# Transfers of 106 rows split into 96 and 10, the input loaded in three parts, edge columns and one-hots moved

## The reference, cut to what matters

```python
def _rgcn_conv(x, edge_index, edge_type, W, root, bias):
    src, dst = edge_index
    x_src = x[src]
    out = x @ root + bias
    for r in range(4):
        mask = (edge_type == r).astype(x.dtype)
        s = segment_sum(x_src * mask[:, None], dst, num_segments=6250)
        c = segment_sum(mask, dst, num_segments=6250)
        out = out + (s / jnp.maximum(c, 1.0)[:, None]) @ W[r]
    return out
# three layers, relu after the first two; then
x = layernorm(x + network(x))
```

## Time and profile before

| | |
|---|---|
| median of 3 runs | 2091.7 us (2090.06 to 2094.24) |
| the profiled execution, its time | 2091.99 us |
| its span | 2090.2 us |
| granted clock of TensorE, mean | 0.879 |
| busy: TensorE, VectorE, ScalarE, GpSimd | 1652.7, 1359.6, 1141.2, 1480.7 us |
| GpSimd's share of the chain that ended last | 40% |

### The profile page before, as it was taken

The page is one execution under the profiler, slowest core; times in us unless marked ns, Lnnn a source line. Parts: engine busy times, 40 slices in busy tenths (PEclk is TensorE's granted clock), DMA queues, the critical chain, the costliest instruction groups (busy, mean ns, idle before and its releaser), DMA issues.

```text
span 2090.2 us, 29086 instructions
## 1 busy us (share of the span) xinstructions
PE 1652.7 (79%) x8296; PEld 1169.6 (56%) x8296; DVE 1359.6 (65%) x4230; ACT 1141.2 (55%) x1679; POOL 1480.7 (71%) x1459
## 2 busy tenths in 40 slices
PE   6702657788899999769999988987769999997743
PEld 3402544344456666547876655655458777775543
DVE  4797866799999988424259988876234252446752
ACT  4511000144566788367858768776367677664500
POOL 1088778877777777647777777777377777777774
PEclk9955666799999999889999999999879999999855
DMA  6411222133344455487855445444488777763431
GB/s 204 159 34 34 72 61 64 58 127 104 124 140 147 157 175 188 135 276 248 269 161 172 169 146 177 159 160 162 139 274 261 236 247 249 238 217 105 142 89 51
DMA packets 169224, 330.76 MB, mean 158 GB/s; under 512 B 34704, under 2 KB 85648, under 8 KB 169060
## 3 DMA queue, kind: packets, MB, share of 16 engines
q1 hardware_dynamic: 119000, 230.27, 31.8%
q0 software_dynamic: 46400, 94.97, 16.2%
q10 hardware_dynamic: 3660, 3.60, 0.7%
HBM read 210.05 MB, written 118.65 MB: 157 GB/s over the span
## 4 chain that ended last, share of the span: by engine, by line
POOL 40%; DVE 21%; PE 18%; issue 14%; DMA 3%; DVEq 1%; ACTq 1%; ACT 1%; SPq 0%; POOLq 0%
POOL ring L796 40%; DVE V L1505 5%; DVE S L1452 4%; PE psB L1043 4%; PE psD L1043 3%; DVE V L1504 3%; DMA ring<-ytab,idxc 2%; PE psY L838 2%; PE psGR L961 2%; PE psRB L961 1%; DVE rows L1300 1%; DVE node L1474 1%; DVEq L1460 1%; DMA hrows<-yst 1%; PE psT L838 1%
## 5 line engine op out<-in xcount | busy, mean ns | idle before, releaser
L796 POOL DMA_INDIRECT ring<-ytab,idxc x1402 | 1410.5, 1006 | 576.1 <-issue 419.7
L1043 PE MATMUL psD<-afull,xs 128*128 128x512 f32 (+1 forms) x1862 | 618.6, 459 | 30.3 <-ACT afull L1128 11.8
L1452 DVE TENSOR_SCALAR S<-odd_f,relc,wc 128x129 f32<-128x129 f32 x1450 | 480.6, 398 | 29.3 <-PE psGR L961 20.3
L1128 ACT ACTIVATE afull<-aring 128x1024 fp32r<-128x1024 f16 (+1 forms) x375 | 367.3, 1032 | 126.5 <-PE psD L1043 54.9
L1043 PEld LDWEIGHTS psD<-afull,xs 128*128 128x128 f32 (+1 forms) x1862 | 359.5, 198 | 96.3 <-ACT afull L1178 20.0
L1505 DVE TENSOR_SCALAR V<-odd_h,recs 128x513 f16<-128x513 f16 x686 | 325.0, 474 | 0.0
L961 PE MATMUL psRB<-S,ring 128*128 128x128 f32 (+1 forms) x1440 | 224.6, 305 | 102.6 <-DMA ring<-ytab,idxc 90.5
L1178 ACT ACTIVATE afull<-psT 128x512 fp32r<-128x512 f32 x355 | 205.2, 593 | 179.6 <-PE psT L1059 177.7
L1182 ACT ACTIVATE aring<-afull 128x1024 f16<-128x1024 f32 x275 | 286.1, 1040 | 25.5 <-ACT afull L1178 0.7
L961 PE MATMUL psGR<-S,ring 128*128 128x128 f32 x1364 | 212.4, 306 | 102.3 <-DMA ring<-ytab,idxc 93.0
L961 PEld LDWEIGHTS psRB<-S,ring 128*128 128x128 f32 (+1 forms) x1440 | 205.3, 214 | 131.6 <-issue 86.4
(11 more groups left out here) (207 smaller groups left out, 1580.8 us busy)
## 6 DMA issues: line engine op xcount, KB each, us to landing
aring<-a_dram SPq DMA_DIRECT2D x180, 512.0 KB
a_dram<-aring SPq DMA_DIRECT2D x132, 512.0 KB
ytab<-yst SPq DMA_DIRECT2D x144, 256.0 KB
ring<-ytab,idxc POOLq DMA_INDIRECT x1402
hrows<-yst SPq DMA_DIRECT2D x96, 64.0 KB
yst<-hrows SPq DMA_DIRECT2D x24, 256.0 KB, 4.6
yst<-in_x SPq DMA_DIRECT2D x23, 256.0 KB, 4.2
out<-yst SPq DMA_DIRECT2D x11, 256.0 KB, 2.7
```

Of the source, the lines that this page charges most:

```text
L796: e.indirect_dma_start(rows_at(n, i, m), None, Y[li % 2], bass.IndirectOffsetOnAxis(ap=idxc[0:m, t:t + 1], axis=0)).then_inc(landed(n), 16)
L1043: last = e.matmul(bank[:], xs[0:m, s, i, :], a, start=(i == 0 and s == 0), stop=(i == NB - 1 and s == 1))
L1128: e.activation(afull[:, n % AF, 0:m, :], aring[:, cc % AS, o:o + m, :], ACT.Copy).then_inc(q["s_cv"], 1)
L1452: last = e.tensor_scalar(run3(S[:, n % NS, i, 0:P + 1]), odd128f, relc[:, t:t + 1], wc[:, t:t + 1], ALU.is_equal, ALU.mult)
```

## The change

- Each transfer of 106 rows (stores of the table and of `hrows`, loads of x, stores of the output) is made in two: rows 0 to 95 and rows 96 to 105 (`row_parts`, `z_moves`).
- x is loaded in three parts: blocks 0 to 7 and 8 to 19 by ScalarE's queue, blocks 20 to 47 and the 106 rows by SyncE's, after the edges and ahead of the constants. The biases have a semaphore of their own, and ScalarE does a small copy right after the identity has landed.
- Edge columns are turned after blocks 0, 2 and 4. TensorE's products for phase 0 come after block 17, the transposes of the edge scans' ends after block 28, the places of phase 0 after block 39, the carries after block 41. VectorE does the edge scans' first half before the scan of phase 0. Phase i+1 is counted before the places of phase i are taken.
- The mask of phase 0 lies in the gather ring, so GpSimd's first gather also waits for the scan of phase 0.
- `ohs` is built for four pairs by one `tensor_tensor` in f16 (by its columns interleaved by four), `ohk` as before. `recs` is split in two tensors.
- START_PE goes from 205 to 177, START_POOL from 95 to 89.

```diff
-START_PE, START_POOL = 205.0, 95.0
+START_PE, START_POOL = 177.0, 89.0
...
+    batch_of, batches = {}, []
+    for v, (w, _, _) in enumerate(pairs):
+        if not batches or len(batches[-1]) == 4 or pairs[batches[-1][0]][0] != w:
+            batches.append([])
+        batch_of[v] = (len(batches) - 1, len(batches[-1]))
+        batches[-1].append(v)
...
+        mask0 = ring[:, 0:(scn + 1) // 2].bitcast(F16)
...
-        nxt0 = min(8, NB - 2)
+        nxt0, nxt1 = min(8, NB - 3), min(20, NB - 2)
+        row_parts = lambda m: [(a, b) for a, b in ((0, m // 16 * 16), (m // 16 * 16, m)) if b > a]
...
-            e.dma_start(Y[li % 2][NR * P * k:NR * (P * k + bw[k]), :].rearrange("(n r) f -> n (r f)", r=NR),
-                        yst[0:bw[k], n % YS, 0:NR * D]).then_inc(s_yd[n % YS], 16)
+            for a, b in row_parts(bw[k]):
+                e.dma_start(Y[li % 2][NR * (P * k + a):NR * (P * k + b), :].rearrange("(n r) f -> n (r f)", r=NR),
+                            yst[a:b, n % YS, 0:NR * D]).then_inc(s_yd[n % YS], 16)
...
 def sync_engine(e):
             load_tail(e, a_typ, typ, q["s_e0"])
+            k = N // P
+            e.dma_start(xn[:, nxt1:k, :], x[nxt1 * P:k * P, :].rearrange("(k p) f -> p k f", p=P)).then_inc(q["s_x2"], 16)
+            for a, b in row_parts(N - k * P):
+                e.dma_start(xn[a:b, k, :], x[k * P + a:k * P + b, :]).then_inc(q["s_x2"], 16)
             e.dma_start(iota[:], c_iota).then_inc(q["s_k0"], 16)
...
 def gpsimd_engine(e):
             e.wait_ge(q["s_tev"], 1)
+            e.wait_ge(q["s_prod"], 1)
             y_stored(e, 0)
...
 def tensor_engine(e):
-            e.wait_ge(q["s_w0"], 48)
+            e.wait_ge(q["s_w0"], 32)
...
+                if k == 0:
+                    pe_cols(e, a_idx, ("s_idx", 1))
                 if k == min(2, NB - 1):
-                    pe_cols(e, a_idx, ("s_idx", 1))
-                if k == min(6, NB - 1):
                     e.wait_ge(q["s_tev"], 1)
                     pe_cols(e, a_dstf, ("s_dst", 1))
-                if k == min(8, NB - 1):
+                if k == min(4, NB - 1):
                     e.wait_ge(q["s_tev"], 2)
                     pe_cols(e, a_rel, ("s_dst", 1))
-                if k == min(24, NB - 1):
+                if k == min(17, NB - 1):
                     pe_rank(e, 0)
-                if k == min(40, NB - 1):
+                if k == min(28, NB - 1):
+                    e.wait_ge(q["s_tev"], 3)
+                    e.wait_ge(q["s_end"], 1)
...
+                if k == min(39, NB - 1):
                     pe_places(e, 0)
+                if k == min(41, NB - 1):
...
 def scalar_engine(e):
-            e.dma_start(bt[:], biases.rearrange("l o -> o l")).then_inc(q["s_w0"], 16)
-            nf = N // P
-            e.dma_start(xn[:, nxt0:nf, :], x[nxt0 * P:nf * P, :].rearrange("(k p) f -> p k f", p=P)).then_inc(q["s_x1"], 16)
-            if nf < NB:
-                e.dma_start(xn[0:bw[-1], NB - 1, :], x[nf * P:N, :]).then_inc(q["s_x1"], 16)
+            e.dma_start(bt[:], biases.rearrange("l o -> o l")).then_inc(q["s_b"], 16)
+            e.dma_start(xn[:, nxt0:nxt1, :], x[nxt0 * P:nxt1 * P, :].rearrange("(k p) f -> p k f", p=P)).then_inc(q["s_x1"], 16)
+            e.wait_ge(q["s_c"], 16)
+            e.activation(sd[:, 0:1], ident[:, 0:1], ACT.Copy)
...
 def vector_engine(e):
             rank_counts(0)
...
-            rank_scan(0)
-            records()
-            rank_places(0)
...
             e.sem_inc(q["s_end"], 1)
+            rank_scan(0)
             e.wait_ge(q["s_tp"], 4)
...
             e.sem_inc(q["s_car"], 1)
+            records()
+            rank_places(0)
             e.wait_ge(q["s_tp"], 5)
...
-            for i in range(1, len(pl.phases)):
-                rank_counts(i)
-                rank_scan(i)
-                rank_places(i)
+            for i in range(1, NPH + 1):
+                if i < NPH:
+                    rank_counts(i)
+                if i > 1:
+                    rank_places(i - 1)
+                if i < NPH:
+                    rank_scan(i)
...
 def onehots(upto):
-                    e.tensor_scalar(run3(ohs[:, v % NO, :]), odd128, recs[:, 0, at:at + 1], None, ALU.is_equal)
-                    e.tensor_scalar(run3(ohk[:, v % NO, :]), odd512, recs[:, 1, at:at + 1], None, ALU.is_equal
+                    if not first:
+                        m = len(batches[n])
+                        e.tensor_tensor(ohs[:, n % NQ, :, 0:m], by4(irep[:, 0:4 * P])[:, :, 0:m],
+                                        recr[:, at:at + m].unsqueeze(1).to_broadcast([P, P, m]), ALU.is_equal)
+                    e.tensor_scalar(run3(ohk[:, v % NO, :]), odd512, reck[:, at:at + 1], None, ALU.is_equal
                                     ).then_inc(q["s_oh"], 1)
```

More of the change, by code:

```diff
@@ L639, in z_plan @@
             for b, ks in enumerate(lasts):
-                parts = 1 if (bw[ks[-1]] == P or len(ks) == 1) else 2
+                parts = len(z_moves(ks))
                 total[b % NZ] += 16 * parts
@@ L677, in x_load @@
                     e.wait_ge(q["s_xw"], n - YS + 1)
-                for a, c, rr in z_parts(ks):
-                    e.dma_start(yst[0:rr, n % YS, a * P:c * P].rearrange("p (k f) -> p k f", f=D),
-                                node_rows(h_dram[l], ks[a], c - a, rr)).then_inc(s_xs[n % YS], 16)
+                for a, c, r, s in z_moves(ks):
+                    e.dma_start(yst[r:s, n % YS, a * P:c * P].rearrange("p (k f) -> p k f", f=D),
+                                node_rows(h_dram[l], ks[a], c - a, r, s)).then_inc(s_xs[n % YS], 16)
             y_stored(e, 0)
@@ L718, in store @@
                     e.wait_ge(q["s_no"], b + 1)
-                    for a, c, rr in z_parts(it[1]):
-                        e.dma_start(node_rows(out, it[1][a], c - a, rr), zx[0:rr, b % NZ, a:c, :]).then_inc(s_z[b % NZ], 16)
+                    for a, c, r, s in z_moves(it[1]):
+                        e.dma_start(node_rows(out, it[1][a], c - a, r, s), zx[r:s, b % NZ, a:c, :]).then_inc(s_z[b % NZ], 16)
                     if b + NZ - 1 < len(lasts):
@@ L1058, in pe_chunk @@
                     e.wait_ge(q["s_oh"], v + 1)
-                    e.matmul(tbank(u)[:], ohs[:, v % NO, 0:P], ohk[:, v % NO, 0:NR * P], start=(j == 0),
+                    e.matmul(tbank(u)[:], ohs[:, batch_of[v][0] % NQ, :, batch_of[v][1]], ohk[:, v % NO, 0:NR * P], start=(j == 0),
                              stop=(j == c - 1)).then_inc(q["s_bd"], 1)
@@ L1500, in onehots @@
                     w, i, j = pairs[v]
-                    if v >= NO:
-                        e.wait_ge(q["s_bd"], v - NO + 1)
                     at = pl.slot0[w] + i * pl.win[w][2] + j
-                    e.tensor_scalar(run3(ohs[:, v % NO, :]), odd128, recs[:, 0, at:at + 1], None, ALU.is_equal)
-                    e.tensor_scalar(run3(ohk[:, v % NO, :]), odd512, recs[:, 1, at:at + 1], None, ALU.is_equal
+                    used = v - NO + 1
+                    n, first = batch_of[v]
+                    if not first and n >= NQ:
+                        used = max(used, batches[n - NQ][-1] + 1)
+                    if used > 0:
+                        e.wait_ge(q["s_bd"], used)
+                    if not first:
[3 more added lines that the diff above has]
+                    e.tensor_scalar(run3(ohk[:, v % NO, :]), odd512, reck[:, at:at + 1], None, ALU.is_equal
                                     ).then_inc(q["s_oh"], 1)
```

75 lines of the change are left out of this document (41 added, 34 removed).

## The result

The changed kernel takes 2058.3 us in the median of four runs (2056.5 to 2060.2), the kernel before 2091.4 beside it; the ratio is 0.984, with a 95% interval from 0.9826 to 0.9854. The forecast was 2079.6, with a range from 2065 to 2093. The direction was right; the gain of 33 us is nearly three times the forecast's 12, and the time lies outside the range.

A forecast was written before the change was run, and what follows sets the result against it. GpSimd's gathers, 1.25 us each at best, with the first gather's time, their stretching, two layer gaps and the tail set the time: -4.0 -4.2 -7.3 -8.2 -1.0 +12.6 = -12.1, so 2079.6 us beside the median, range 2065 to 2093.

The forecast's parts named there:

- First gather, -8.2: Start of the kernel: GpSimd's first gather moves from 100.68 to about 92.5 us, -4.0 and -4.2.
- Its two parts: Before the first gather: (a) the split store of the 106-row block, -4.0; (b) blocks coming earlier, -4.2.
- Edge scans, -7.3: First gathers: VectorE's edge scans come earlier and stretch fewer gathers, -7.3 us, between -3 and -7.9.
- the gathers up to 124.9 would lie near 945: Sign at the start of layer 0: these gathers, 1510 ns in the mean before, would take near 945 ns.
- Gaps, -8.2: Two gaps between layers: split 106-row stores save 4.2 us in the first, 4.0 in the second; from -3 to -9.
- the shifted planner constants: Order of layer 0: worth 0, with -3 to +3 for output blocks more or fewer after its last gather.
- Tail, -1.0: End of the kernel: the output's last 106-row transfer is split, -1.0 us, from 0 to -1.8.
- One-hots, +12.6: Gathers: 179 new tensor_tensor hold them 0.07 us each, +12.6 us in all; ends +3 and +25.
- VectorE is relieved of 114 us, off the path: worth 0: VectorE: one-hots fall from 189 us to 75 us, and this relief changes nothing in the time.
- Rival 1: Gathers: the new tensor_tensor hold hardly any, 0.02 us each, +3.5 in all; time 2071 us; chance 19%.
- Waits in layer 0, 0: GpSimd in layer 0: no term for waits for others; gathers waiting elsewhere would show the forecast wrong.
- The expected rise between 400 and 880 us: Gathers from 400 to 880 us: longer by some 7 us in sum, as 392 of the 686 pairs are there.

The follow-up runs named there:

- e4: The changed kernel with every 106-row transfer whole again: 2075.0 us (0.992).
- e9: The changed kernel with each of the first four tensor_tensor of a `bins` group waited for before the next is issued: 2019.4 us (0.9662).
- e1: The changed kernel with both one-hots made by tensor_scalar again, as in the kernel before: 2057.8 us (0.9843).
- e2: The kernel before with only the new one-hots of four pairs: 2090.9 us (1.0005).
- e8: The changed kernel with START_PE and START_POOL put back to 205 and 95: 2064.0 us (0.9869).
- e3: The kernel before with only START_PE and START_POOL of the changed kernel (177 and 89): 2088.1 us (0.9985).
- e13: The changed kernel with one wait in a `bins` group, behind its first instruction: 2024.6 us (0.9681).
- e5: The changed kernel with the batched one-hot made by a tensor_scalar of one SBUF input, that part of the output not the reference's: 2050.9 us (0.9805).
- e10: e9 with both one-hots by tensor_scalar again, as in e1: 2031.2 us (0.9714).
- e6: The changed kernel with the load of input blocks 20 to 48 issued from GpSimd's queue, behind its memsets, not SP's: 2066.6 us (0.988).

## Why the prediction was wrong, step by step

- **First gather, -8.2: right.** -8.8, and each of its marks (block 0, block 4, the last block) came within 1.6 us. Its two parts can't be told apart: e4, with whole transfers, starts at 94.3, which is 2.4 behind the changed kernel and 5.1 behind e9 (91.9, 89.3 and 89.2 in the changed kernel, e1 and e9, with the same start), where the forecast had 4.0.
- **Edge scans, -7.3: right** in size: 7.3 to 0.4. That the gathers up to 124.9 would lie near 945 was wrong: the ranking moved up too, and its scan holds the gather at 118.84 for 10.62 us. In sum the ranks cost what they did (29.4 for 30.8).
- **Gaps, -8.2: mis-sized.** -12.9, beyond the term's bound of -9. The split's part at the first gap was 5 for 4.2. What failed is "So 0 [...] also for the shifted planner constants": the three blocks fewer behind the last gather, which the forecast knew only as a bound of -3 to +3, were there, and brought 3 us.
- **Tail, -1.0: right**, -0.8.
- **One-hots, +12.6: the step that failed, though its number is right.** 13.5 us of holds, by the mechanism as told, from instructions of 485 ns and not 419. "VectorE is relieved of 114 us, off the path: worth 0" is the false sentence. The busy time fell by 53 us only (1359.6 to 1306.7), and it was not worth 0: with the batches the groups of `bins` hold the gathers 7 us (e2), 9.5 (e1) or 11 (the whole change) less, and the time is the same with the new one-hots as without. I had the row of these groups and used it only to price the new instructions. Rival 1 had the right total for the one-hots for a wrong reason, and even it gives 2071.
- **Waits in layer 0, 0:** 3.0 us went. e1 and e8 have none either, nor do e2 and e3, so no single part is needed for it. There is only one trace of the kernel before, and what removed its three waits stays open.
- **The expected rise between 400 and 880 us didn't come.** The groups of the gathers over 480 us that begin 299 us after the first gather, first before (400 to 880), then changed (391 to 871):

```profile
L796 POOL DMA_INDIRECT ring<-ytab,idxc x365 | 367.0, 1005 | 114.2 <-issue 108.5 <-PE psGR L961 3.4 <-PE psRB L961 2.3
```

```profile
L821 POOL DMA_INDIRECT ring<-ytab,idxc x361 | 359.7, 996 | 110.0 <-issue 108.2 <-PE psGR L992 0.9 <-PE psRB L992 0.9
```

Their excess fell by 3.5 us where 7 more were forecast.

The ends of the range counted the unpriced relief as zero from both sides; with -11 for it, -3 for the order and -3 for the waits the sum would have been 2063.

**What stays open.** That a pause inside a group makes its hold short is shown (e9, e13). Why the gathers meet the groups later where the one-hots are batched is not. The meeting points do bunch: in 7 of the 26 groups directly behind a one-hot, a gather reaches its moment 0.55 us into the group, and in each of them the gather before it had met a batch. But e5, whose batches hold next to none, shows the relief too. Nor do the traces show what in VectorE or GpSimd keeps the gather out through a run, or why a group directly behind an addition lets it in.

## What to carry over

An engine off the critical path isn't free to be changed: when its instructions can hold those of the engine that sets the time, price how the others it runs will meet them too, and try the part alone in both surroundings. Where one engine's instructions stretch another's, look at the runs, not at single ones: a short pause of VectorE behind the first of five two-input instructions was worth 34 us here (e13), one behind each of the first four 39 (e9). Before a difference of 2 us between two traces is given to an edit, look at how far kernels with the same part differ there. And a relief that is worth nothing today may be the next bound's only room (12 us, e10 against e9).

## What the hardware showed that I had not expected

- A gather that meets a run of VectorE instructions with two SBUF inputs is held to the end of the run when VectorE came into the run straight from a one-hot, S or a rectifier (2.17 us for a gather of 0.945), but only to the end of one instruction when a pause precedes it, or an addition of a sum (0.22 us at most behind 11 such additions before). The Trainium skill, page "SBUF — State Buffer", section "Who interferes with whom", has the one that issues first keep the shared ports for its whole instruction. The trace agrees with that for a single instruction (0.16 us in e9's rows); that the hold can go on through all that follow in a run of five is the measurement's.
- The same batch by one SBUF input (e5) holds next to nothing: 1.4 against 13.5 us.
- A small transfer beside a large one: the 1.5 KB of biases landed 14.5 us after their issue when GpSimd's queue carried the large load (e6), 8.7 when the load stood behind the edges in SP's queue. The constants moved too, so that the load did it is not shown alone.
